# The closing stage of a routed feed-forward layer, cut into half batches on two DMA queues

## The reference, cut to what matters

```python
x = x + attention(layernorm(x))            # 16 heads, causal scores without softmax
xm = layernorm(x).reshape(-1, 128)
probs = softmax(xm @ Wg)                   # 8 experts
p, e = top_k(probs, 2)                     # two experts of each token
y[token, k] = p[token, k] * (relu(xm @ W1[e] + b1[e]) @ W2[e] + b2[e])
out = x + y[:, 0] + y[:, 1]
```

## Time and profile before

| | us |
|---|---|
| median of the timed runs (3) | 309.36 |
| lowest and highest | 308.80 and 309.73 |
| span of the profiled execution, first to last instruction | 350.7 |
| first load of the closing stage issued (L289), in the span | 330.14 |

### The profile page before, as it was taken

The page is one execution under the profiler, slowest core; times in us unless marked ns, Lnnn a source line. Parts: engine busy times, 40 slices in busy tenths (PEclk is TensorE's granted clock), DMA queues, the critical chain, the costliest instruction groups (busy, mean ns, idle before and its releaser), DMA issues.

```text
span 350.7 us, 6314 instructions
## 1 busy us (share of the span) xinstructions
PE 234.8 (67%) x1320; PEld 174.7 (50%) x1320; DVE 207.1 (59%) x745; ACT 140.9 (40%) x509; POOL 198.4 (57%) x184
## 2 busy tenths in 40 slices
PE   0799999999998999574300685977677686665000
PEld 0345666666565655363100675976567685554000
DVE  6888887989898989654541043434333443343074
ACT  2434566566565554342200363444343544342000
POOL 3465644588888888744673045554564455646300
PEclk9999999999999999855555599689898989999555
DMA  7910000000010101101121332223223232201199
GB/s 218 304 57 0 3 0 3 3 31 30 31 33 30 33 30 33 53 31 38 39 84 60 72 99 70 71 71 76 68 72 84 62 78 65 81 28 39 50 358 317
DMA packets 32399, 25.48 MB, mean 73 GB/s; under 512 B 4305, under 2 KB 30169, under 8 KB 32364
## 3 DMA queue, kind: packets, MB, share of 16 engines
q1 hardware_dynamic: 23808, 14.52, 15.2%
q0 software_dynamic: 4320, 8.47, 7.6%
q10 hardware_dynamic: 4236, 2.10, 2.0%
HBM read 13.92 MB, written 11.61 MB: 73 GB/s over the span
## 4 chain that ended last, share of the span: by engine, by line
issue 52%; PE 27%; DMA 5%; SPq 4%; ACT 3%; DVE 2%; ACTq 1%; another core or an unknown queue 1%; POOL 1%; DVEq 1%; POOLq 0%
PE ps L824 14%; PE ps L832 9%; PE ps L817 4%; DMA back<-returned 3%; ACT hT L458 3%; SPq L271 2%; SPq L289 2%; DMA bias_bc<-b_o 1%; DMA returned<-y_sb,xt 1%; POOL outer L324 1%; DMA xt<-dispatched 1%; DMA dispatched<-padding 1%; PE ps L709 0%; DVEq L243 0%
## 5 line engine op out<-in xcount | busy, mean ns | idle before, releaser
L349 POOL DMA_INDIRECT returned<-y_sb,xt x71 | 70.2, 988 | 70.9 <-DVE y_sb L685 51.3
L324 POOL TENSOR_TENSOR outer<-qkv 128x1024 f32<-128x1024 f32 x32 | 62.6, 1957 | 32.4 <-ACT qkv L404 32.0
L340 POOL DMA_INDIRECT dispatched<-rows,slot x64 | 62.5, 976 | 25.1 <-issue 15.4
L680 DVE TENSOR_TENSOR yb<-ps,b_bc 128x128 f32<-128x128 f32 x71 | 20.7, 291 | 77.2 <-PE ps L832 32.8
L824 PE MATMUL ps<-xT,w_of 128*128 128x128 f32 x284 | 51.1, 308 | 18.7 <-ACT hT L458 12.5
L739 PE MATMUL ps<-outer,causal 128*128 128x512 f32 x128 | 62.4, 610 | 0.0
L832 PE MATMUL ps<-w_sb,hT 128*128 x284 | 50.0, 304 | 16.3 <-ACT hT L458 10.3
L452 ACT ACTIVATE xT<-ps 128x128 f32<-128x128 f32 x71 | 19.8, 279 | 91.7 <-PE ps L817 72.1
L824 PEld LDWEIGHTS ps<-xT,w_of 128*128 128x128 f32 x284 | 42.8, 216 | 23.0 <-ACT xT L452 16.4
L832 PEld LDWEIGHTS ps<-w_sb,hT 128*128 128x128 f32 x284 | 42.3, 214 | 20.1 <-issue 19.9
L458 ACT ACTIVATE hT<-ps,b_col 128x128 f32<-128x128 f32 x142 | 44.4, 370 | 4.7 <-remote 3.0
(11 more groups left out here) (115 smaller groups left out, 355.5 us busy)
## 6 DMA issues: line engine op xcount, KB each, us to landing
xt<-dispatched SPq DMA_DIRECT2D x71, 65.0 KB
back<-returned SPq DMA_DIRECT2D x8, 512.0 KB, 7.6
x_sb<-x SPq DMA_DIRECT2D x8, 256.0 KB, 5.2
out<-x_sb ACTq DMA_DIRECT2D x8, 256.0 KB, 6.6
returned<-y_sb,xt POOLq DMA_INDIRECT x71, 2.3
w_sb<-w SPq DMA_DIRECT2D x1, 1024.0 KB, 5.6
w_sb<-w SPq DMA_DIRECT2D x2, 512.0 KB, 7.2
dispatched<-rows,slot POOLq DMA_INDIRECT x64
```

What stands on the lines that cost most here:

```text
L324: pool.tensor_tensor(outer[:, g % OUTER_RING, :].rearrange("p (h b a) -> p h b a", h=HEADS, b=DH), k, v, ALU.mult).then_inc(outer_done, 1)
L340: pool.indirect_dma_start(out=dispatched[:, :], out_offset=bass.IndirectOffsetOnAxis(ap=slot[:, g * K + k:g * K + k + 1], axis=0), in_=row ...
L349: pool.indirect_dma_start(out=returned[:, :], out_offset=bass.IndirectOffsetOnAxis(ap=xt[:, n % G, D:D + 1].bitcast(I32), axis=0), in_=y_s ...
```

## The change

Each batch is cut into two halves of two tiles. The loads of the first halves stay on the sync queue, the loads of the second halves go to ScalarE's queue, which now also waits for the sixteen `return_done` semaphores. VectorE adds two tiles at a time, in sixteen steps of two instructions of 128 by 256 elements, and there are sixteen `back_in` semaphores. The stores of the first halves are issued by the sync queue behind its eight loads, those of the second halves by ScalarE's queue behind its eight loads. Every row of memory is still read and written once, in runs of the same length.

```diff
--- before.py
+++ after.py
@@ -204,9 +204,9 @@
         TX_done, xT_done, w1_done, h_mm, hT_done, y_mm, yb_done, y_done = (
             sem("TX_done"), sem("xT_done"), sem("w1_done"), sem("h_mm"), sem("hT_done"), sem("y_mm"), sem("yb_done"), sem("y_done"))
         return_done = [sem(f"return_done{t}") for t in range(G)]
-        back_in = [sem(f"back_in{b}") for b in range(B)]
+        back_in = [sem(f"back_in{i}") for i in range(2 * B)]
         first_added, both_added = sem("first_added"), sem("both_added")
-        stored = sem("stored")
+        stored_sp, stored_act = sem("stored_sp"), sem("stored_act")
 
         def tile(g):
             return x_sb[:, g * P:(g + 1) * P]
@@ -232,6 +232,14 @@
 
         N_FILLS = 6
         N_CONSTS = 8
+        def back_half(b, half):
+            at = (2 * b + half) * T * D
+            return back[:, at:at + T * D].rearrange("p (t f) -> p t f", t=T // 2)
+
+        def x2_half(b, half):
+            at = (2 * b + half) * (T // 2) * D
+            return x_sb[:, at:at + (T // 2) * D].rearrange("p (t d) -> p t d", t=T // 2)
+
         block = ctx.enter_context(nc.Block())
 
         def apart(eng):
@@ -286,9 +294,12 @@
             for t in range(G):
                 sp.wait_ge(return_done[t], 16 * returns(t))
             for b in range(B):
-                sp.dma_start(back[:, b * T * K * D:(b + 1) * T * K * D].rearrange("p (t f) -> p t f", t=T),
-                             back_t[b]).then_inc(back_in[b], 16)
-            sp.wait_ge(stored, 16 * B)
+                sp.dma_start(back_half(b, 0), back_t[b, :, 0:T // 2, :]).then_inc(back_in[2 * b], 16)
+            for b in range(B):
+                sp.wait_ge(both_added, 2 * b + 1)
+                sp.dma_start(out_t[b, :, 0:T // 2, :], x2_half(b, 0)).then_inc(stored_sp, 16)
+            sp.wait_ge(stored_sp, 16 * B)
+            sp.wait_ge(stored_act, 16 * B)
 
         @block.gpsimd
         def _(pool):
@@ -460,9 +471,13 @@
 
             tile_slots([(1, xT_out), (3, hT_out), (-3, bias_registers)], BLOCKS)
 
+            for t in range(G):
+                act.wait_ge(return_done[t], 16 * returns(t))
             for b in range(B):
-                act.wait_ge(both_added, b + 1)
-                act.dma_start(out_t[b], x_sb[:, b * T * D:(b + 1) * T * D].rearrange("p (t d) -> p t d", t=T)).then_inc(stored, 16)
+                act.dma_start(back_half(b, 1), back_t[b, :, T // 2:T, :]).then_inc(back_in[2 * b + 1], 16)
+            for b in range(B):
+                act.wait_ge(both_added, 2 * b + 2)
+                act.dma_start(out_t[b, :, T // 2:T, :], x2_half(b, 1)).then_inc(stored_act, 16)
 
         @block.vector
         def _(dve):
@@ -686,13 +701,12 @@
 
             tile_slots([(5, y_out), (6, y_weighted), (0, w1_out), (-3, registers)], BLOCKS)
 
-            for b in range(B):
-                x2_b = x_sb[:, b * T * D:(b + 1) * T * D].rearrange("p (t d) -> p t d", t=T)
-                y_b = back[:, b * T * K * D:(b + 1) * T * K * D].rearrange("p (t k d) -> p t k d", t=T, k=K)
-                dve.wait_ge(back_in[b], 16)
-                dve.tensor_tensor(x2_b, x2_b, y_b[:, :, 0, :], ALU.add).then_inc(first_added, 1)
-                dve.wait_ge(first_added, b + 1)
-                dve.tensor_tensor(x2_b, x2_b, y_b[:, :, 1, :], ALU.add).then_inc(both_added, 1)
+            for i in range(2 * B):
+                y_i = back[:, i * T * D:(i + 1) * T * D].rearrange("p (t k d) -> p t k d", t=T // 2, k=K)
+                dve.wait_ge(back_in[i], 16)
+                dve.tensor_tensor(x2_half(i // 2, i % 2), x2_half(i // 2, i % 2), y_i[:, :, 0, :], ALU.add).then_inc(first_added, 1)
+                dve.wait_ge(first_added, i + 1)
+                dve.tensor_tensor(x2_half(i // 2, i % 2), x2_half(i // 2, i % 2), y_i[:, :, 1, :], ALU.add).then_inc(both_added, 1)
 
         @block.tensor
         def _(pe):
```

## The result

| | before | changed |
|---|---|---|
| median of 13 timed runs, us | 308.97 | 310.70 |
| lowest and highest, us | 308.47, 310.62 | 309.25, 312.34 |
| ratio to before, 95% interval | | 1.0044 (1.0025 to 1.0063) |
| span of the profiled execution, us | 350.7 | 310.6 |
| stage in the trace: first load's issue to the end of the span, us | 20.58 | 21.65 |

What follows compares the result with a forecast made beforehand. The prediction took the closing stage as bound by 4.19 MB in and 2.10 MB out on 16 DMA engines. All terms were nothing except transfer order, +0.33 us, giving 309.36 + 0.3 = 309.7 us, range 308.3 to 311.0.

Steps and rivals of the forecast that it cites:

- the forecast's own range of 309.2 to 310.2: Range around 309.7 us for the main case, loads then stores and DMA-bound, given a chance of 0.42.
- The start: Closing stage's first load issue: stays about 0.4 us behind the last scatter's landing, no effect.
- The ramp at nothing: First 1.5 us of loads at 84 GB/s: two queues change nothing, taken as 0 with bounds 0 and -1.2 us.
- Order of loads and stores, +0.33: Closing stage's transfers: loads alone at 350 GB/s, then stores alone at 343, losing the turns at 370; +0.33 us.
- third rival: Loads and stores on the two queues still take turns at 370 GB/s, stage ends as before: 309.4 us; chance 0.12.
- The reading of 379 and 350 GB/s: Closing stage's loads: 379 GB/s until VectorE's sums begin, 350 with loads alone beside the sums.
- first rival: Two queues move more than one, both phases at 370 GB/s: about 308.4 us (308.2 to 308.8); chance 0.26.
- Sums of two tiles: VectorE's half-batch sums: 428 ns each, 0.81 us a half, 13.0 us for sixteen against 10.7, covered by DMA.
- second rival: VectorE becomes the bound from 0.89 us a half on; 311.2 us at 0.99 a half, 310.4 at 0.94; chance 0.20.
- the sixteen more sums, put at nothing on the path: VectorE in the closing stage: +2.3 us of work from halving, yet VectorE does not pass the DMA.
- cover of 1.3 us for the last store: End of the stage: last sum forecast at 347.3 us, may end as late as 348.6 without delaying the last landing.

Runs made afterwards that it cites:

- e2: Kernel before, but whole batches on two queues: even batches on the sync queue, odd on ScalarE's, stores behind loads; ratio 1.0012, stage 20.96 us.
- e7: Kernel before without the closing stage's sums, stores issued at once on ScalarE's queue beside the sync queue's loads; last landing 20.10 us behind the first issue.
- e8: Changed kernel without the sums, stores issued straight behind the loads on both queues; last landing 20.58 us behind the first issue.
- the rounds without a fetch: Rounds 2 and 3 of e11 and e12, with no instruction fetch in either kernel; they show 0.15 and 0.35 us for order and halving.
- e3: Changed kernel with 28 idle semaphore increments on VectorE ahead of its sums, so the fetch comes before the stage; ratio 1.0010, stage 21.02 us.
- e1: Changed kernel's half batches and smaller sums, but all loads on the sync queue and all stores on ScalarE's; ratio 1.0033 to before, stage 20.91 us.
- e5: e1 with 28 idle increments on VectorE ahead of the sums, so the fetch comes before the stage; ratio 0.9981 to before, stage 21.50 us.
- e11: Kernel before with its closing stage run five times in a row, each after the previous one's last store landed; 390.36 us, ratio 1.2634.
- e12: Changed kernel with its closing stage run five times in a row; 393.75 us, ratio 1.2734 to the kernel before.
- e6: Kernel before with 4 idle increments on VectorE ahead of its sums; the fetch stayed behind the stage; ratio 0.9974, stage 20.51 us.
- e4: Kernel before with 10 idle increments on VectorE ahead of its sums; the fetch came ahead of the stage; ratio 0.9983, stage 20.66 us.
- e10: Kernel before with 7 idle increments on VectorE ahead of its sums; the fetch came ahead of the stage; ratio 0.9997, stage 20.70 us.

## Why the prediction was right, and where it was off

The prediction gave 309.7 us with a range of 308.3 to 311.0; the changed kernel takes 310.7. The sign is that of the forecast, the size is three to four times as large (+0.33 forecast, +1.07 in the trace, +1.36 timed). The time lies outside the forecast's own range of 309.2 to 310.2, and the stage of 21.65 us is over the 21.5 at which the prediction called itself wrong. So the wide range held, and the sum did not. Step by step:

- *The start.* The first issue 0.4 us behind the last scatter's landing: it is 288.96 against 288.59. Right.
- *The ramp at nothing.* 74 GB/s for 1.3 us, as before. Right; in this trace two queues don't start faster.
- *Order of loads and stores, +0.33.* The order came as described, at 351 and 343 GB/s. By e2 it costs 0.33 us; with halving, by e7 and e8 0.48 and by the rounds without a fetch 0.15 to 0.35. Right in place, and in size as far as single traces tell. The first 512-byte packet at 13.5 us, behind the 10.9 at which the third rival would have shown, rules that rival out.
- *The reading of 379 and 350 GB/s.* I took the fall to come with the sums. e8 shows it without any. It did not enter the sum, but it was wrong, and with it my argument that a lone queue doesn't cap at 350; what refutes the first rival is that two queues run at 351 and 343 too. The Trainium skill, page "DMA: Bandwidth & Descriptors", section "Issuing engines are not separate DMA queues", says that all issuers share the same 16 DMA engines. The trace agrees: 351 GB/s on two queues, 350 on one.
- *Sums of two tiles.* 428 ns and 0.81 us a half forecast; 0.42 to 0.43 and 0.79 measured. The last sum ends 16.9 us behind the first issue, forecast 17.2, and its store then takes 4.2 us to land, behind other stores. VectorE is not the bound, and the second rival fell, though the result lies on its side.
- *The term that was mis-sized: the sixteen more sums, put at nothing on the path.* Their time is indeed covered. But they are also sixteen more instructions in VectorE's stream, which bring an 8 KB fetch into the stage, and one late DMA engine then sets its end. By e3 this is +0.63 us in the trace, the larger part of the loss. Nor did the prediction allow for a DMA that lands late by one engine: its cover of 1.3 us for the last store was reckoned against the DMA engines all together.

Together 0.38 (e2's stage) + 0.06 (e3 above e2) + 0.63 (changed above e3) = 1.07 us in the trace. The sum closes by construction, since each term is the difference of two neighbours, and each comes from single traces, which differ by up to 0.2 us for the same stage: the 0.63 stands clear of that, the 0.38 barely, the 0.06 not. The timed loss of 1.36 with its interval of 0.8 to 1.9 holds 1.07; whether the remaining 0.3 is real isn't settled. That 310.7 lies within the range is luck: its upper end was carried by a rival that has nothing to do with the cause.

## What to carry to other kernels

When a stage keeps all 16 DMA engines busy, as here, don't expect splitting its transfers over more queues to move bytes sooner; ask instead whether reads and writes still take turns, and don't let the writes starve the reads on which the end depends. A DMA lands when its slowest engine does, so compare the completions of its engines: one that is late from a certain moment on can point to something else that this engine did, though e1 shows late ones without a fetch. Count instructions as well as their time: moved into the stretch ahead of the stage, where the DMA engines are mostly idle, the fetch cost nothing measurable, and inside the saturated stage it cost 0.4 to 0.9 us in all traced stages that held one but e1's.

## What the runs showed of the hardware

- Reads of 1 KB runs from HBM alone: 379 to 386 GB/s for 1 to 2 us, then about 350, in 512 KB loads on one queue or two and in 256 KB loads on two, with or without sums beside them. In 256 KB loads on one queue: 317 (e1), and 225 to 337 in e5; why is open. Writes of 512-byte runs alone: 343. Both in turns: 370.
- One 8 KB instruction fetch beside saturated DMA engines: in the changed kernel, in round 1 of e11 and in rounds 1 and 5 of e12, one of the sixteen completions is 0.5 to 1.0 us behind the others in every load that lands more than 1 us after it. In the changed order it is so again in the last store (0.50 to 0.65 us); in the old order it reaches the end through the late last load. In e1 it is 0.2 to 0.4 us and gone by the last stores.
- The end of a program can be set by the DMA engines while the chain of waits names another: here its last 4.9 us are VectorE's sums, and that they are not the bound is seen only in the last store's 4.2 us to landing.
- The same kernel before took 309 us on two chips and 350.57 us on a third, timed without a trace. The prediction took the 41 us between the span and the timed runs for a possible effect of the trace; the changed kernel's span of 310.6 us and e6's of 349.9 us on that third chip say that a trace adds no such thing. The profile of before looks like one from a chip like the third, by its span and by its mean granted clock of 0.854 (0.860 in e6 there, 0.876 to 0.885 in the one-stage kernels on the other chips); on which chip it was taken isn't known. The stage is not touched by it: 20.58 us in that profile and 20.51 in e6, 20.66 and 20.70 in e4 and e10 on the other chips.
